# One graph layer on one core: where in VectorE's and ScalarE's step x2 and z2 are made, and a pipeline one step shorter

## What is computed

```
h    = relu(layernorm(x))                                 # x: 50000 x 128
xn   = layernorm(h, g1, b1)
msg  = relu(xn[src] + edge_attr)                          # 25000 edges
aggr = segment_sum(msg, dst)
g    = relu(((1 + eps) * xn + aggr) @ Wg1 + bg1) @ Wg2 + bg2
x2   = h + g
f    = gelu(layernorm(x2, g2, b2) @ Wf1 + bf1) @ Wf2 + bf2   # 128 -> 512 -> 128
out  = x + x2 + f
```

## Time and profile before

| | |
|---|---|
| median of 3 runs | 1067.87 us (1066.06 to 1068.01) |
| the profiled execution, its own time | 1065.76 us |
| its span, first to last instruction | 1064.0 us (1.76 us of the time lie outside) |
| PE busy | 992.4 us, 93% |
| DVE busy | 978.6 us, 92% |
| ACT busy | 844.1 us, 79% |
| POOL busy | 800.9 us, 75% |
| granted TensorE clock | 0.979 on average, 1.00 from 100 us on |

### The profile page before, as it was taken

The page is one execution under the profiler, slowest core; times in us unless marked ns, Lnnn a source line. Parts: engine busy times, 40 slices in busy tenths (PEclk is TensorE's granted clock), DMA queues, the critical chain, the costliest instruction groups (busy, mean ns, idle before and its releaser), DMA issues. The chain is left out here.

```text
span 1064.0 us, 23086 instructions
## 1 busy us (share of the span) xinstructions
PE 992.4 (93%) x6684; PEld 852.4 (80%) x6684; DVE 978.6 (92%) x3499; ACT 844.1 (79%) x2158; POOL 800.9 (75%) x510
## 2 busy tenths in 40 slices
PE   1456999999999999999999999999999999999998
PEld 0345888888888888888888888888888888888887
DVE  5679999999999999999999999999999999998752
ACT  1247888888888888888888888888888888878773
POOL 6588878878878778878878878878878878876610
PEclk9758999999999999999999999999999999999999
DMA  7565667778887555554554564654654654443311
GB/s 262 165 182 136 185 177 182 211 223 236 250 229 196 142 140 114 146 140 114 146 140 113 147 140 113 146 140 113 147 139 112 146 140 114 115 109 92 59 57 40
DMA packets 110468, 156.87 MB, mean 147 GB/s; under 512 B 24835, under 2 KB 50607, under 8 KB 110334
## 3 DMA queue, kind: packets, MB, share of 16 engines
q1 hardware_dynamic: 70358, 128.99, 37.4%
q0 software_dynamic: 37760, 25.66, 19.4%
q10 hardware_dynamic: 2216, 0.66, 0.3%
HBM read 90.61 MB, written 64.61 MB: 146 GB/s over the span
## 5 line engine op out<-in xcount | busy, mean ns | idle before, releaser
L521 ACT ACTIVATE n_act<-p_f,bf1e_col 128x512 f32<-128x512 f32 x392 | 255.9, 679 | 149.6 <-PE p_f L882 144.8
L926 PE MATMUL p_out<-wf,n_act 128*128 128x128 f32 x3136 | 370.5, 276 | 0.0
L446 POOL DMA_INDIRECT aggr_sums<-e_merged,e_index x196 | 323.7, 1652 | 59.7 <-issue 49.9
L926 PEld LDWEIGHTS p_out<-wf,n_act 128*128 128x128 f32 x3136 | 357.7, 191 | 3.9
L455 POOL TENSOR_TENSOR n_rstd<-n_var,minus_half 128x12 f32<-128x12 f32 (+2 forms) x102 | 256.6, 2515 | 114.5 <-DVE n_var L829 57.8
L435 POOL DMA_INDIRECT e_x<-in_x,e_cols x196 | 214.7, 1095 | 60.1 <-issue 59.1
L882 PE MATMUL p_f<-n_z2T_high,wf_low 128*128 128x512 f32 x392 | 207.5, 529 | 10.7 <-issue 6.7
L882 PE MATMUL p_f<-n_z2T_high,wf_high 128*128 128x512 f32 x392 | 155.2, 396 | 0.0
L882 PE MATMUL p_f<-n_z2T_low,wf_high 128*128 128x512 f32 x392 | 154.4, 394 | 0.0
L674 DVE BATCH_NORM_STATS2 n_stat<-n_x 128x6 f32<-128x256 f32 x392 | 139.6, 415 | 0.1
L571 ACT ACTIVATE n_relu<-n_x,n_minus 128x128 f32<-128x128 f32 x392 | 124.7, 396 | 12.5 <-DVE n_minus L812 12.5
(11 more groups left out here) (85 smaller groups left out, 1432.5 us busy)
## 6 DMA issues: line engine op xcount, KB each, us to landing
n_x<-in_x SPq DMA_DIRECT2D x97, 256.0 KB
n_aggr<-aggr_sums SPq DMA_DIRECT2D x97, 256.0 KB
out_dram<-n_out SPq DMA_DIRECT2D x97, 256.0 KB
aggr_sums<-zeros SPq DMA_DIRECT2D x26, 512.0 KB, 5.8
e_dst<-in_dst_rows SPq DMA_DIRECT2D x49, 256.0 KB
e_attr<-in_attr SPq DMA_DIRECT2D x48, 256.0 KB
aggr_sums<-zeros SPq DMA_DIRECT2D x12, 1024.0 KB
e_x<-in_x,e_cols POOLq DMA_INDIRECT x196
```

The lines of the kernel that those rows point to most:

```text
L446: nc.gpsimd.indirect_dma_start(out=aggr, out_offset=bass.IndirectOffsetOnAxis(ap=e_index[0:r, s, j:j + 1], axis=0), in_=e_merged[0:r, s, j ...
L521: nc.scalar.activation(n_act[:, k, :, 0:b.rows], p_f[k % 2][:, :, 0:b.rows], ACT.Gelu, bias=bf1e_col[:, k:k + 1]).then_inc(s_act, 1)
L926: last = nc.tensor.matmul(p_out[0:b.rows, j, :], n_act[:, k, j, 0:b.rows], wf2[:, k, :], start=False, stop=(k == KF - 1), skip_group_check ...
```

## The change

The two lags are one smaller (`NODE_LAG` 7 to 6, `SP_LAG` 9 to 8). `x2`, its statistics and its variance are made in DVE step b+3, in the middle and behind the product of the same step, and no longer at the start of step b+4. `n_z2` is made in ACT step b+4 in the middle, between gelu 2 and gelu 3, and is transposed in PE's same step, between the second and third part of the second product; `z2T_high` and `z2_low` follow in step b+4. The first product, the gelus, the second product and `n_out` of a block stand one step sooner.

DVE's step begins with `n_out`, `n_in`, the seed of `p_out`. Small operations that depend on the one ahead of them get other work between. ACT's order of a step becomes: gelu 0, seeds (0, 1), gelu 1, seeds (2, 3), `hidden`, gelu 2, in odd steps `merged_rows`, then `n_z2`, gelu 3, `n_relu`, `z2T_high`, in even steps `e_msg`, `n_inT`, in even steps `e_relu`. PE's order becomes: first product 0, 1; `p_g`; first product 2, 3; `p_in`; `p_gout`; second product 0, 1; `p_z2`; second product 2, 3; in even steps `p_merged`. POOL's text is not touched.

```
-NODE_LAG = 7
-SP_LAG = 9
+NODE_LAG = 6
+SP_LAG = 8
...
# ScalarE's step
                     seed_gout(b, (0, 1))
-                if 1 in halves and 0 not in halves:
-                    merged_rows(edge(3))
-                if (b := node(6)) is not None:
+                if (b := node(5)) is not None:
                     gelu(b, 1)
                 if (b := node(3)) is not None:
+                    seed_gout(b, (2, 3))
                     hidden(b)
-                    seed_gout(b, (2, 3))
...
+                if (b := node(5)) is not None:
                     gelu(b, 2)
-                    gelu(b, 3)
...
+                if 1 in halves and 0 not in halves:
                     merged_rows(edge(3))
                 if (b := node(4)) is not None:
...
                         last = nc.scalar.activation(n_z2[0:r, b.slot(2), j, :], n_x2[0:r, b.slot(4), j, :],
                                                     ACT.Identity, scale=n_rstd[0:r, after_three(b), 2, j:j + 1])
                     last.then_inc(s_z2, 1)
+                if (b := node(5)) is not None:
+                    gelu(b, 3)
+                if (b := node(0)) is not None:
...
+                        last = nc.scalar.activation(n_relu[0:r, b.slot(4), j, :], n_x[0:r, b.slot(8), j, :], ACT.Relu,
...
+                if (b := node(4)) is not None:
+                    act.wait_ge(s_tz2, b.at + 1)
...
+                if 0 in halves and (c := edge(3)) is not None:
+                    act.wait_ge(s_esum, c.at + 1)
...
# VectorE: new functions, called in the middle of first_half and second_half
+            def second_norm(node):
+                if (b := node(3)) is not None:
+                    r = b.rows
+                    dve.wait_ge(s_gout, b.at + 1)
+                    reached(dve, s_z2, b.at - 3)
+                    nc.vector.tensor_tensor(n_x2[0:r, b.slot(4)], p_gout[0:r], bias_of(0, r),
+                                            ALU.add).then_inc(s_x2, 1)
+
+            def second_stats(node):
+                if (b := node(3)) is not None:
+                    dve.wait_ge(s_x2, b.at + 1)
+                    stats(n_stat2[:, b.slot(8)], n_x2[:, b.slot(4)], b.rows, s_stat2)
+
+            def second_variance(node):
+                if (b := node(3)) is not None:
...
# TensorE's step
+            def second_product(b, ks):
+                for k in ks:
+                    pe.wait_ge(s_act, b.at * KF + (k + 1))
+                    for j in range(J):
+                        last = nc.tensor.matmul(p_out[0:b.rows, j, :], n_act[:, k, j, 0:b.rows], wf2[:, k, :],
...
+                if (b := sixth) is not None:
+                    second_product(b, (1,))
+                if (b := fifth) is not None:
+                    pe.wait_ge(s_z2, b.at + 1)
...
+                if (b := sixth) is not None:
+                    second_product(b, (2, 3))
```

More of the change, by code:

```diff
@@ L620, in _ @@
             half_chunk(step)
[L621 removed]
+            branch(act, EDGE_LAG, 5, step)
         @block.vector
@@ L684, in z2_low @@
             def z2_low(node):
-                if (b := node(5)) is not None:
+                if (b := node(4)) is not None:
                     dve.wait_ge(s_z2T, b.at + 1)
@@ L725, in first_half @@
                     reached(dve, s_emm, c.at - 2)
[L726 to L734, removed]
+                    matches(c, 0)
+                second_variance(node)
+                z2_low(node)
+                relu_stats(node)
+                if c is not None:
+                    matches(c, 1).then_inc(s_ematch, 1)
                 variance_of(node)
@@ L769, in second_half @@
                                             ALU.max).then_inc(s_eindex, 1)
+                second_stats(node)
+                if c is not None:
                     if c.is_number(0):
@@ L793, in second_half @@
                     last.then_inc(s_esum, 1)
+                variance_of(node)
             def step(node, edge, halves, apart):
-                first, third, fifth = node(0), node(2), node(4)
-                if (b := fifth) is not None:
+                first, third, fourth = node(0), node(2), node(3)
+                if (b := node(6)) is not None:
                     r = b.rows
[L799 to L814, removed]
+                    dve.wait_ge(s_fout, b.at + 1)
+                    if not (b.fixed and b.k < 2):
+                        dve.wait_ge(q_out[b.slot(2)], 16 * b.uses(2))
+                    nc.vector.tensor_tensor(n_out[0:r, b.slot(2)], p_out[0:r], bias_of(1, r),
+                                            ALU.add).then_inc(s_nout, 1)
                 if (b := third) is not None:
@@ L843, in step @@
                                             ALU.add).then_inc(s_x2b, 1)
+                if (b := first) is not None:
+                    dve.wait_ge(q_x[b.slot(8)], 16 * (b.uses(8) + 1))
+                    stats(n_stat[:, b.slot(8), 0], n_x[:, b.slot(8)], b.rows, s_nstat)
                 if (b := node(1)) is not None:
@@ L850, in step @@
                     last.then_inc(s_nzg, 1)
+                if (b := first) is not None:
+                    r, s = b.rows, b.slot(8)
+                    dve.wait_ge(s_nstat, b.at + 1)
+                    nc.vector.tensor_scalar(n_minus[0:r, s], n_stat[0:r, s, 0, :, 1], -1.0, None,
+                                            ALU.mult).then_inc(s_nminus, 1)
+                    variance0_of(node)
                 if 0 in halves or not halves:
```

109 lines of the change are left out of this document (57 added, 52 removed).

## The result

The changed kernel takes 1099.09 us (median of 4 runs, 1098.06 to 1106.33) against 1067.91 us before: a ratio of 1.0311, with a 95% interval of 1.0265 to 1.0357. It is slower, which was forecast; the forecast of 1080 us and its range up to 1094 were too low. The profiled execution has a span of 1096.3 us, 32.3 more than before.

What follows compares the result with a forecast made beforehand. DVE bounds the kernel before at 20.03 us a pair; a new loop through POOL sets 20.49. 41 pairs give +18.9, the start 0, the drain -7.0: +11.9 us, 1077.7 on the profiled execution, forecast 1080, range 1055 to 1094.

Steps and rivals of the forecast that it cites:

- What bounds the kernel now: In the kernel before, DVE, issuing instruction after instruction without waiting for another engine, sets a pair of steps at 20.03 us.
- 19.67: DVE's cost of a pair in us once two waits of 0.18 us for its own results are gone from 20.03.
- The ring: Loop per pair: p_merged, gelu 0, merged_rows, POOL's scatters, gathers and power, n_z2, e_msg, next p_merged; 20.49 us, setting the pace.
- Link 4: From the end of merged_rows to POOL's first scatter, POOL sitting waiting: taken as 0.88 us, other bound 0.20.
- the way to gelu 0: First link of the ring, from the even step's first p_merged matmul to gelu 0: 2.24 us.
- the way from `e_msg` to `p_merged`: Last link of the ring, from ACT's e_msg to PE's next p_merged: taken as 0.03 us.
- link 8: Link of the ring from the end of POOL's power to ACT's n_z2: 0.03 us.
- A late gather would stall DVE, but DVE has 0.82 us of slack: DVE's even step wants gathered rows about one and a half us sooner; slack 20.49 - 19.67 per pair, costed at nothing.
- slower still: Rival: handovers between engines take longer or a gather lands late; 0.4 us more per pair, about 1096 us, chance 0.12.
- The start: First stretch of the run: DVE has idle time and takes the earlier work in it, costed at 0.
- The drain: End of the run, going through PE: one step of 7.0 us fewer, so -7.0 us.
- Dependent operations apart: In DVE's step, four n_in between n_out and the seed of p_out remove two waits of 0.18 us per pair.

Runs made afterwards that it cites:

- e4: Kernel before with n_out moved ahead of n_in in DVE's step, nothing else: 1061.0 us, ratio 0.9938.
- e10: Kernel before with n_out ahead of n_in and merged_rows behind gelu 1: 1060.5 us, ratio 0.9939.
- e2: Changed kernel with POOL's two gathers ahead of its two scatters in the odd step only: 1074.7 us, ratio 1.0076.
- e11: Changed kernel with POOL's gathers ahead of its scatters in both steps: 1045.8 us, ratio 0.9773.
- e1: Changed kernel with merged_rows put back directly behind the first two seeds in ACT's odd step: 1055.3 us, ratio 0.9885.
- e3: Changed kernel with e_msg put ahead of n_z2 in ACT's even step, the copy staying late: 1089.8 us, ratio 1.0214.
- e5: Kernel before with merged_rows moved from behind seeds (0, 1) to behind seeds (2, 3): 1066.2 us, ratio 0.9988.
- e8: Changed kernel with the second part of the zero-fill of aggr_sums given out at half the rate: 1097.2 us, ratio 1.0284.

## Why the prediction was wrong in size

**What bounds the kernel now: right, but with a neighbour.** DVE set the 20.03 us, and e4 took 0.22 us off by one reordering. The 19.67 that I took for DVE alone was not reached in the kernel before, where PE's list with its one wait for ACT stands at 19.81 (e4, e10). It was passed in the new order: 19.55 (e2, e11), so 19.67 was itself 0.12 too high for DVE. DVE's rows had more small holes than the two that I subtracted: one `e_match` takes 0.45 us to the next instruction before and 0.39 in e11, `e_zg` 1.09 and 1.04.

**The ring: right in every link.** It was forecast at 20.49 us and is 20.64 in the pair shown, 20.67 on average in mid-run. e1, e2 and e3 each cut it at another link, and each time the pair fell. e5 shows that both moves are needed. Link 4, on which the forecast depended, was taken as 0.88 and is 0.87, not the 0.20 behind a power. My reason for it was half right: it is not that POOL comes from idling, for in e1 the scatter is 0.85 behind the copy with the power still running at the copy's end. The 0.20 is seen where the copy ended 3.46 us before the scatter. Against this link I also held a first-byte latency, which ends at the first byte and not at the start of the instruction; it is another interval. The largest misses are two of 0.07 us, the way to gelu 0 (2.31 for 2.24) and the way from `e_msg` to `p_merged` (0.10 for 0.03, which I had copied from link 8 though no row showed this crossing). 0.18 us is nothing in one pair; times 41 it is 7 us.

**"A late gather would stall DVE, but DVE has 0.82 us of slack": the step that failed.** I costed it at nothing without a row for how long a gather takes to land. The slack was there in mid-run, where the pairs are the ring's own. It was not in the first third, where the zero-fill runs: the rows come 6.7 us after the gather began, DVE wants them earlier in its step than before and POOL issues the gathers behind a copy that is later. The pairs there are 6 us longer in all. e1, which brings the gathers forward by the copy's distance, leaves 1.9 of 18.6 us of these waits; e8, with less traffic from 220 us on, leaves 3.1 of 12.0 us there and takes 4 of the 6 us away. That the rest is due to late gathers too is not shown: in e1 too the pairs of the first third lie nearly 3 us in all above its mid-run. My "slower still" rival named a late gather, but as one of several handovers and in all pairs. That its 1096 us are near the measured 1099 is luck: of its 0.4 us a pair the ring took 0.18.

**The start: costed at 0, measured +4.9.** I argued that DVE has idle time there. It has, but it idles for gathers (16.0 us between 30 and 110 us in the changed kernel), and the chain that ended last between 30 and 60 us goes through POOL: 28.2% of it is the landing of gathered rows, 21.8% scatters, 13.0% gathers. So POOL's order moves the start, and the late copy delays POOL there as well. The start is +2.9 in e1, +1.9 in e2 and -1.0 in e11, each read from one execution. So some 2 us of the 4.9 go with the place of the copy; what makes the other 2.9 was not tried.

**The drain: -7.0 forecast, -4.9 measured.** One step is gone, but POOL's last scatters give some back. From the last `p_merged` to the end it is 1064.0 - 984.5 = 79.5 us before and 1096.3 - 1021.3 = 75.0 after the change. There the second pair of scatters waits for the landing of the first, the power stands behind it, and ACT waits for that power at `n_z2`, with PE behind ACT (0.97 us):

```profile
1039.78 2.76 POOL L446 DMA_INDIRECT aggr_sums<-e_merged,e_index  x1 [2.68 <-DMA aggr_sums<-e_merged,e_index]
...
1048.08 1.28 ACT L576 ACTIVATE n_z<-n_x,n_rstd 128x128 f32<-128x128 f32 x4 [2.09 <-POOL n_rstd L455]
```

In the kernel before ACT has no such wait there. With the copy early (e1) the same stretch is 1053.5 - 980.3 = 73.2 us, -6.3 against before, and with the late copy in e11 it is 1045.5 - 970.2 = 75.3. So the late copy costs about 2 us once more.

**Dependent operations apart:** the wait behind `n_out` is gone, as said: in the changed kernel `n_in` follows it after 0.60 us, where the seed followed after 0.79.

```profile
590.33 0.68 DVE L835 TENSOR_TENSOR n_out<-p_out,rows 128x512 f32<-128x512 f32 x1
...
590.93 1.13 DVE L844 SCALAR_TENSOR_TENSOR n_in<-n_zg,n_rstd,n_aggr 128x128 f32<-128x128 f32 x4
```

It shows in the time only once the ring is broken.

Beside the ring's own +18.9, which was forecast, there are 7 us of mis-sized links, 6 in the first third, 5 of the start and 2 of the drain: together 20, the difference between +11.9 and +32.3.

## What to carry to other kernels

- In a pipeline of hand-ordered queues, a move is free only if no ring closes through it. Write the ring down link by link, across all queues, and compare its length with the busiest engine's work per period; two moves that are harmless alone (e5; n_z2 early with the copy early, e1) can close one together.
- Look at what stands behind a waiting instruction on its queue. Here a 0.6 us copy held two scatters, two gathers and a power; swapping gathers and scatters made 53 us of difference to the changed kernel.
- Before a latency is called covered, find a row for it in the stretch with the most traffic, not in mid-run.
- When two engines are both busy for 99% of the time, work out what a period costs the second one too, with its waits. Here that was 19.81 us for PE, and a saving of 0.36 us on DVE alone gave 0.22.

## What the runs showed of the hardware that was not expected

- An indirect DMA of POOL that had waited for ACT's copy began 0.85 to 0.87 us after the copy's end, in all 24 pairs of the changed kernel between 400 and 900 us. That time runs on beside POOL's own work: in e1 it is 0.85 with POOL in a power for the first 0.46 of it, so part of it can be hidden. Where the copy had ended 3.46 us before, the DMA began 0.20 us behind POOL's last instruction.
- The Trainium skill gives about 1 us of first-byte latency on this path ("DMA: Bandwidth & Descriptors", "Specifications"). That ends at the first byte, the 0.87 us end where the instruction begins; no run here shows the skill's figure.
- Gathered rows of 64 KB per instruction (128 rows of 512 bytes) landed 6.7 us after the gather began at 309 us; between 305 and 320 us the core's DMAs, the zero-fill among them, moved 248 GB/s.
